# Two more chunks get their right fields by DMA, and a pair of weight tiles is finished before chunk 4's products

## What is computed

```python
X0 = inputs.reshape(-1, 32, 64)
Xi = X0
pools = []
for W, b in ((W1, b1), (W2, b2), (W3, b3)):
    Wr = W.reshape(128, 32, Xi.shape[1])
    Xi = jnp.einsum('bhd,bmd,ohm->bod', X0, Xi, Wr) + b[None, :, None]
    pools.append(Xi.sum(axis=-1))
return jnp.concatenate(pools, axis=-1) @ fc_W.T + fc_b
```

## Time and profile before

| what | value |
|---|---|
| median of 3 runs | 82.0 us (81.88 to 83.26) |
| the profiled execution's own time | 82.64 us |
| its span, first to last instruction | 80.8 us |
| PE busy | 75.0 us (93%) |
| DVE / ACT / POOL busy | 47.1 / 34.6 / 49.8 us |
| DMA | 12.01 MB, mean 149 GB/s |

### The profile page before, as it was taken

One profiled execution on the slowest core, in us unless ns is written; L12 is line 12 of the kernel. 1 busy time (PEld: TensorE's weight loads), 2 busy tenths in 40 slices (PEclk: granted clock), 3 DMA queues, 4 the chain that ended last, 5 costly groups with the idle time before them and its releaser, 6 DMA issues.

```text
span 80.8 us, 1130 instructions
## 1 busy us (share of the span) xinstructions
PE 75.0 (93%) x372; PEld 51.7 (64%) x372; DVE 47.1 (58%) x44; ACT 34.6 (43%) x51; POOL 49.8 (62%) x49
## 2 busy tenths in 40 slices
PE   4999699989999999959999999999999999999970
PEld 1326255743218677648888888888888888886850
DVE  1056999996797998497499709973003003113541
ACT  1833994579779943983836500580300300000000
POOL 4989836999993699492099989629924103261400
PEclk9999999999999999999999999999999999999999
DMA  0998999999996434369992000000000000000000
GB/s 22 252 366 250 369 370 352 381 385 392 375 322 196 128 89 110 101 215 385 353 417 89 4 4 0 4 0 0 0 0 0 0 0 8 0 0 0 0 0 0
DMA packets 7529, 12.01 MB, mean 149 GB/s; under 512 B 835, under 2 KB 3971, under 8 KB 7267
## 3 DMA queue, kind: packets, MB, share of 16 engines
q1 hardware_dynamic: 6915, 11.16, 40.3%
q10 hardware_dynamic: 608, 0.77, 3.0%
HBM read 10.88 MB, written 1.05 MB: 148 GB/s over the span
## 4 chain that ended last, share of the span: by engine, by line
PE 61%; DMA 14%; SPq 13%; ACT 4%; ACTq 2%; issue 2%; DVE 1%; DVEq 0%
PE a_ps L581 28%; PE x_ps L581 21%; DMA w_sb<-w 14%; SPq L183 6%; SPq L195 3%; SPq L200 2%; ACT feat L360 2%; PE x_ps L601 2%; PE a_ps L628 2%; PE z_ps L575 2%; PE a_ps L627 2%; ACTq L432 2%; PE a_ps L666 1%; PE x_ps L739 1%; ACT zz L360 1%
## 5 line engine op out<-in xcount | busy, mean ns | idle before, releaser
L266 POOL TENSOR_TENSOR feat<-r_in,feat 128x1024 fp32r<-128x1024 f32 x8 | 19.2, 2404 | 4.1 <-ACT feat L360 3.6
L581 PE MATMUL x_ps<-feat,w_hi 128*128 128x512 f32 x64 | 18.8, 393 | 0.0
L504 DVE SCALAR_TENSOR_TENSOR x<-a_ps,vec,x 128x512 f32<-128x512 f32 x7 | 5.3, 751 | 19.2 <-PE a_ps L628 19.1
L581 PE MATMUL a_ps<-feat,a_hi 128*128 128x512 f32 x64 | 16.2, 395 | 0.0
L259 POOL TENSOR_TENSOR xs<-x_in,xs 32x512 fp32r<-32x512 f32 x7 | 10.8, 1548 | 8.1 <-ACT xs L360 7.8
L273 POOL TENSOR_TENSOR x<-x 128x512 f32<-128x512 f32 x6 | 7.8, 1292 | 11.5 <-DVE x L504 11.3
L581 PEld LDWEIGHTS x_ps<-feat,w_hi 128*128 128x128 f32 x64 | 11.9, 188 | 2.6
L581 PEld LDWEIGHTS a_ps<-feat,a_hi 128*128 128x128 f32 x64 | 11.9, 188 | 2.7
L360 ACT ACTIVATE feat<-z_ps 128x1024 fp32r<-128x1024 f32 x8 | 8.2, 1025 | 7.4 <-DVE z_ps L477 6.2
L484 DVE TENSOR_TENSOR feat<-z_ps,feat 128x1024 fp32r<-128x1024 f32 x8 | 9.7, 1218 | 2.1 <-ACT feat L360 2.1
L374 ACT ACTIVATE x<-x_ps,vec 128x512 f32<-128x512 f32 x8 | 5.4, 686 | 12.3 <-PE x_ps L601 12.3
(11 more groups left out here) (76 smaller groups left out, 75.3 us busy)
## 6 DMA issues: line engine op xcount, KB each, us to landing
w_sb<-w SPq DMA_DIRECT2D x9, 512.0 KB, 8.8
x_in<-xl SPq DMA_DIRECT2D x8, 256.0 KB, 7.4
r_in<-xr SPq DMA_DIRECT2D x2, 1024.0 KB, 6.1
a_by_fields<-at_sb SPq DMA_DIRECT2D x8, 96.0 KB, 2.1
x<-x ACTq DMA_DIRECT2D x1, 512.0 KB, 4.6
x<-x SPq DMA_DIRECT2D x1, 512.0 KB, 6.0
w_sb<-w SPq DMA_DIRECT2D x1, 256.0 KB, 11.7
a_by_fields<-at_sb SPq DMA_DIRECT2D x4, 64.0 KB, 2.1
```

The costliest lines, as they stand in the source:

```text
L266: nc.gpsimd.tensor_tensor(feat[:, c, 1, of_half(1), :], z_of(c, 1), feat[:, c, 0, of_half(1), :].bitcast(f32), ALU.subtract).then_inc(lo_d ...
L504: nc.vector.scalar_tensor_tensor(out=x1[:, c, :], in0=a_ps[:, c % 2, :], scalar=vec[:, 3:4], in1=x1[:, c, :], op0=ALU.add, op1=ALU.mult).t ...
L581: nc.tensor.matmul(bank, weights[:, k, :], feat[:, c, part, k, :], start=(start and k == 0), stop=False)
```

## The change

`PICKED` goes from 6 to 4, so the right fields of chunks 4 and 5 are read from DRAM (1 MB each) instead of being made by PE. The eight `pick_right` matmuls for them are gone. SP issues chunk 4's right fields behind W1's last two tiles, ahead of x of chunks 5 and 6; chunk 5's where chunk 6's stood; 6's and 7's follow x of chunk 7, each with a wait that its buffer is free. On DVE `rest_lo` of W1's last tiles goes ahead of chunk 4's products, and chunk 5 goes behind `rest_lo` of A, just ahead of chunk 6. On ACT `split_x(4)`, `hi(5, 0)`, `hi(5, 1)` and `split_x(5)` go behind the copy of q. On POOL `split_x(4)` and `split_x(5)` go behind `lo(4)`.

```diff
-PICKED = 6
+PICKED = 4
...
             def load_right(c):
-                if c % 2 == 0:
+
+                if c == PICKED:
                     sp.wait_ge(spread_done, 3)
                 else:
-                    sp.wait_ge(hi_done, count(PICKED - 1, 1))
-                    sp.wait_ge(lo_done[1], PICKED)
+                    sp.wait_ge(hi_done, count(max(c - 2, PICKED - 1), 1))
+                    sp.wait_ge(lo_done[1], max(c - 1, PICKED))
...
             sp.dma_start(w1_sb[:, :, EVEN:, :], w1[:, :, EVEN:, :]).then_inc(w1_rest_in, 16)
+            load_right(4)
             load_x(5)
             load_x(6)
...
-            load_right(PICKED)
+            load_right(5)
             sp.wait_ge(lo16_done, 1)
...
             load_x(7)
-            load_right(PICKED + 1)
+            load_right(6)
+            load_right(7)
...
             pool.wait_ge(lo_done[1], 2)
-            split_x(4)
-            pool.wait_ge(xs_lo, 5)
             lo(2)
...
             pool.wait_ge(w_sum, 2)
+            lo(3)
+            lo(4)
+            pool.wait_ge(lo_done[1], 5)
+            split_x(4)
             split_x(5)
             pool.wait_ge(xs_lo, 6)
-            lo(3)
-            lo(4)
             lo(5)
...
             hi(2, 0)
-            split_x(4)
             hi(2, 1)
...
-            split_x(5)
             hi(4, 0)
             hi(4, 1)
...
-            hi(5, 0)
-            hi(5, 1)
             save_zz(1)
...
-            split_x(6)
             save_x1(4)
             act.wait_ge(q_ready, 1)
             copy(q_sb[:, :], q_ps).then_inc(q_saved, 1)
+            split_x(4)
+            hi(5, 0)
+            hi(5, 1)
+            split_x(5)
+            split_x(6)
             hi(6, 0)
...
             chunk(3)
-            mult(4, 0)
-            mult(4, 1)
             dve.wait_ge(w_hi_done, 2)
             rest_lo(w1_sb[:, 0, :, :], w1_hi, w_lo_done)
-            lo(4)
-            chunk(5)
+            chunk(4)
...
             rest_lo(f1, a_hi, a_lo_done)
+            chunk(5)
             chunk(6)
...
-            pick_right(4, 0)
             x1_lo(0, 1)
-            pick_right(4, 1)
             x1_hi(1, 0)
             x1_lo(1, 0)
             x1_hi(1, 1)
-            pick_right(5, 0)
             x1_lo(1, 1)
             x1_tail(0)
             x1_tail(1)
-            pick_right(5, 1)
             spread16(1)
```

More of the change, by code:

```diff
@@ L470, in mult @@
                 else:
-                    dve.wait_ge(r_here[c % 2], 16)
+                    dve.wait_ge(r_here[c % 2], 16 * ((c - PICKED) // 2 + 1))
                     right = r_in[:, c % 2, tiles, :]
```

## The result

The changed kernel takes 87.39 us (86.97 to 87.86, four runs) against 81.94 for the one before: a ratio of 1.066, interval 1.060 to 1.071. I had forecast 85.2 with a range to 87.2, so the sign was right and the time lay outside. The profiled execution has a span of 86.1 against 80.8. The medians of the experiments leave out executions over 1.5% longer than the fastest of their kernel; the ranges in brackets keep them.

A forecast was written before the change was run, and what follows sets the result against it. It took the start of tail 2, after ACT's chain of waits, and then PE's matmuls with operands ready in time as the bound; 0.6 + 0.7 + 0.6 + 1.3 = +3.2 us on the median 82.0 gave 85.2, range 82.8 to 87.2.

The forecast's parts named there:

- the weighing of the clock: PE before X1 of chunk 2: rival that 2.7 us idle brings back half pace, 2.3 us more, 87.5; chance 0.07.
- Matmuls of 0.44 us behind 32: Sign of being wrong: PE matmuls at the 1.2 GHz pace after 32 us, against 0.23 us at 2.4 GHz.
- Eight matmuls fewer: PE before tail 0: 1.85 us less work, which becomes idle time, about 2.7 us before X1 of chunk 2.
- rest_lo: DVE, W1's last tiles: waits for POOL's lo(3) to 28.5, ends at 28.8; being made ahead gives nothing.
- Chunk 4 behind it, tail 2 at 35.8 (+0.6): Chunk 4's products follow rest_lo, delaying hi(4, 1) and ACT's saves; tail 2 at 35.8 against 35.24, +0.6 us.
- The transfers, cost 0 to 1: Chunk 4's 1 MB lands at 26.8, before DVE asks; cost 0, at most 1 if chunk 5's transfer slips.
- Behind q, 0.7, 0.6 and 1.3: PE waits for lo(5) 0.7 us, for lo(6) 0.6, and for save_x1(5) before X1 of chunk 7 1.3.
- the prediction's second case: If chunk 6's right fields land behind POOL's split, turns swap: PE waits 2.3 us for product(0), sum +2.9.
- Both operands in SBUF: DVE instructions with both operands in SBUF and POOL's take turns; chunks 4 and 5 products now read SBUF, against the change.
- The back half absorbs it: Rival behind q: without the turns lo(5) ends 1.2 us before it is wanted; +0.6, 82.6 us; chance 0.14.
- faster: Rival: rest_lo and chunk 4's products unhindered by POOL, tail 2 1.6 us earlier; -1.6, 80.4 us; chance 0.07.
- late transfer: Rival: chunk 4's right fields land at 30.1, 1.3 us behind DVE's request, delaying tail 2; 86.5 us; chance 0.05.

The follow-up runs named there:

- nine matmuls: Changed kernel plus nine matmuls of unused result in PE's idle time between spread16(1) and X1 of chunk 2: 85.6 us, profiled execution 85.12.
- the pair: Changed kernel with x splits and sums early and product(0) ahead of chunk 6: 85.07 us; the second adds nine unused matmuls in PE's idle time: 82.79 us.
- the saves first: Changed kernel with ACT's save_x1(0) and save_x1(1) ahead of hi(4, 0) and hi(4, 1): 86.07 us.
- POOL held back: Changed kernel with POOL's lo(3) waiting until both products of chunk 4 are made: 85.77 us.
- four matmuls: Changed kernel plus four matmuls of unused result in PE's idle time between spread16(1) and X1 of chunk 2: 86.21 us.

## Why the prediction was wrong, point by point

The measured +5.3 of the span comes out of the rows. PE reached the end of X1 of chunk 4 at 44.23 in place of 41.54: +2.7; by the trace with nine matmuls 2.4 of it are the half rate (X1 of chunk 2 in 5.28 against 2.87) and 0.3 the later start. Then X1 of chunk 5 took 54.46 - 50.91 = 3.55 where 2.99 is its own: +0.6. X1 of chunk 6 took 61.58 - 57.67 = 3.91: +0.9. A of chunk 3 and the wait behind it took 65.76 - 61.58 = 4.18 where 3.21 is its own: +1.0. That is 5.1; the last 0.1 to 0.2 is beyond X1 of chunk 7.

**The step that failed** is the weighing of the clock: the main sum put this term at nothing, and it measured 2.3 us. The idle time was right (2.7 forecast, 2.47 measured), and so was the price that the rival gave: "11 x 0.21 = 2.3 us", "85.2 + 2.3 = 87.5", where 2.3 and 87.39 were measured. But it stood among the rivals with 0.07, on the ground that 0.97 us of idle time had done nothing, and that none of 2.7 was shown. Idle time almost three times as long as that wasn't bounded by those rows, and the term should have been in the main sum or at even odds; the range then would have reached 88. That the price fits so well is in part luck: it took over the 11 slow matmuls from the kernel's start, and no row said that the half rate would last as long here (12 matmuls in the trace, and less in the executions of the shorter kind). Matmuls of 0.44 us behind 32, named ahead as a sign of being wrong, are in the trace (5.28 / 12). The nine matmuls and the pair show the mechanism: same start, full clock, 2.3 us less. The Trainium skill, "TensorE: Matmul & The Clock Gate", "HAM oscillation — how this bites in real kernels", gave the rule that idle gaps of PE drop it to half rate. The runs agree that a gap does it, and decide on its size: one of 2.47 us was enough, shorter than those that the page warns of, while gaps of 1.55 and 1.80 didn't.

*Eight matmuls fewer*: right, they became idle time. *rest_lo*: right. 2.46 us, 0.3 behind `lo(3)`, and 0.42 once POOL is held back. Alone in the kernel before it still costs 1.2 us, by the wait for ACT's copy; I had seen no price in that, as I looked only at what comes behind it.

*Chunk 4 behind it, tail 2 at 35.8 (+0.6)*: a bit too dear. At full rate X1 of chunk 2 from 32.63 would have had its tail at 35.5, +0.3.

*The transfers, cost 0 to 1*: right for the changed kernel, whose slow front hides them. Wrong as a general statement: where q came 4.1 and 4.5 us earlier (the saves first, POOL held back), DVE waited for both of them, and the waits behind q grew by 2.1 and 2.6 us. The four matmuls' trace has no such wait; its front had lost 1.1 us elsewhere.

*Behind q, 0.7, 0.6 and 1.3*: measured 0.6, 0.9 and 1.0, in the places and by the releasers forecast; 2.6 against 2.5. But they arose with q 2.7 us later, not 0.6. At full clock the order can be another: in the trace with nine matmuls chunk 6's right fields come behind the start of POOL's split, and PE waits for `product(0)`. That is the swap of turns of the prediction's second case, with 1.73 us where it said 2.3, and 85.12 us for that execution. Repairing the waits (the pair's first against the changed kernel) gave 2.3.

*Both operands in SBUF*: this spoke against the change, but in the changed kernel the four products of chunks 4 and 5 met no instruction of POOL and took 1.23 or 1.24 us each. The turns came from `rest_lo` beside `lo(3)`, and from chunk 6's products (2.32, and 2.19 in the earlier trace rows) now that POOL's split and `lo(5)` run beside them.

*The rivals.* "The back half absorbs it" and "faster" are out by the same rows, and so is the late transfer: DVE's first product of chunk 4 follows `rest_lo` at once, 28.42 behind 28.38. For the first it matters that the waits behind q do absorb, in the other direction: gains of the front.

## What to carry to other kernels

Work taken off a waiting engine becomes idle time, and on PE idle time can cost more than itself: where a change opens a gap longer than any in the trace, the clock belongs in the sum, and the granted clock per stretch shows it, not the busy share. Before an operand moves from PSUM to SBUF, or a DVE instruction with two SBUF operands to another place, look at what POOL runs then, as the two take turns: `rest_lo` of 0.42 us became 2.46, and with ACT's saves first the second product of chunk 5, 1.22 us when it read PSUM, took 2.19. When several causes stand in a row, repair them together before pricing one: alone, each repair here gave back 1.2 to 1.8 us by the medians, of gains up to 4.5 at q.

## What the runs showed of the hardware that I had not expected

The clock had already fallen inside a gap of 2.47 us (0.83 as the mean over 30 to 32 us) and stayed at half for some 5 us of full work from 32.6 on; gaps of 1.80 and 1.55 left it at 1.00. The half-rate stretch at 12 to 16 us in one variant's trace came without any gap above 1.2 us, after 4 us in which PE was busy a little over half of the time; in the changed kernel's trace PE was about as busy there (0.94 and 1.54 of two stretches) and the clock stayed full. What sets it off wasn't tried. What exactly besides the length of a gap decides, such as the 1.14 us of idle time shortly before it, stays open too: the kernel with four matmuls had it ahead of a gap of 1.55 us and kept its clock, and no kernel had the long gap without it.
